# One-hots from a row of 2-byte integers, and the skip projection made in the attention layer's node step

## What is computed

```python
# attention layer: x1 is its result, a row of 256 for each node
x1 = segment_sum(h[src] * alpha[:, :, None], dst, n).reshape(n, H * C1) + gat_bias
x1 = prelu(x1, prelu1_a)
# transformer layer
q = x1 @ Wq + bq;  k = x1 @ Wk + bk;  v = x1 @ Wv + bv
logits2 = einsum("ec,ec->e", q[d2], k[s2]) / 16
alpha2 = segment_softmax(logits2, d2, n)
out = segment_sum(v[s2] * alpha2[:, None], d2, n)
out = out + x1 @ Wskip + bskip
x = x + prelu(out, prelu2_a)
```

## Time and profile before

| | us |
|---|---|
| median of 3 runs | 4608.18 |
| lowest and highest | 4602.61, 4608.73 |
| the profiled execution, its own time | 4611.11 |
| its span | 4609.2 |
| PE, DVE, ACT, POOL busy in it | 3524.1, 2667.7, 742.4, 3235.1 |
| granted TensorE clock, mean | 0.871 |

### The profile page before, as it was taken

The page is one execution under the profiler, slowest core; times in us unless marked ns, Lnnn a source line. Parts: engine busy times, 40 slices in busy tenths (PEclk is TensorE's granted clock), DMA queues, the critical chain, the costliest instruction groups (busy, mean ns, idle before and its releaser), DMA issues. The chain is left out here.

```text
span 4609.2 us, 73629 instructions
## 1 busy us (share of the span) xinstructions
PE 3524.1 (76%) x14587; PEld 2499.9 (54%) x14588; DVE 2667.7 (58%) x10225; ACT 742.4 (16%) x2298; POOL 3235.1 (70%) x3404
## 2 busy tenths in 40 slices
PE   2366666666566666666679999999978899999998
PEld 2244444444344444444456666666656676676666
DVE  8544444444333433344368888887866776776765
ACT  3200000000011111111111111111112322322322
POOL 3477777777677777777677777777727777777762
PEclk7677877777788989989878898999978999999999
DMA  5544444444444444444455555555525555555552
GB/s 165 133 129 132 130 129 131 131 128 129 114 139 136 138 137 138 139 134 138 120 143 155 150 156 151 154 152 155 150 83 141 159 154 152 160 147 145 153 146 73
DMA packets 339313, 639.35 MB, mean 139 GB/s; under 512 B 85419, under 2 KB 218598, under 8 KB 338790
## 3 DMA queue, kind: packets, MB, share of 16 engines
q0 software_dynamic: 159744, 440.25, 35.8%
q1 hardware_dynamic: 159993, 180.48, 12.4%
q10 hardware_dynamic: 19056, 12.87, 1.0%
HBM read 569.33 MB, written 63.99 MB: 137 GB/s over the span
## 5 line engine op out<-in xcount | busy, mean ns | idle before, releaser
L582 POOL DMA_INDIRECT g_G<-t,srcI x1664 | 1587.8, 954 | 507.1 <-issue 507.1
L755 PE MATMUL g_ps<-g_G,g_oh 128*128 128x256 f32 x3328 | 1034.0, 461 | 468.9 <-DMA g_G<-t,srcI 364.4
L755 PEld LDWEIGHTS g_ps<-g_G,g_oh 128*128 128x128 f32 x3328 | 727.9, 228 | 741.0 <-issue 404.6
L1472 POOL DMA_INDIRECT g_G<-t,srcI x832 | 798.5, 960 | 287.7 <-issue 253.3
L881 POOL DMA_INDIRECT g_G<-t,srcI x832 | 806.7, 970 | 253.3 <-issue 251.5
L1813 PE MATMUL g_psA<-g_win,g_ohT 128*128 128x257 f32 x1664 | 548.1, 414 | 105.5 <-issue 46.5
L1574 DVE CUSTOM_DVE_ANT_0 g_junk<-g_G,g_psA 128x257 f32<-128x257 f32 x832 | 348.4, 419 | 288.8 <-PE g_psA L1813 265.2
L1823 PE MATMUL g_ps<-g_G,g_oh 128*128 128x257 f32 x1664 | 509.9, 390 | 0.0
L636 DVE TENSOR_SCALAR g_oh<-iota,g_relx,g_wx 128x128 f32<-128x128 f32 x1664 | 452.2, 364 | 59.1 <-PE g_ps L755 34.0
L1245 PE MATMUL g_ps<-g_Gp,g_oh 128*128 128x264 f32 x1664 | 420.5, 403 | 22.3 <-issue 19.2
L1813 PEld LDWEIGHTS g_psA<-g_win,g_ohT 128*128 128x128 f32 x1664 | 293.0, 197 | 214.9 <-DVE g_L L1574 94.7
(11 more groups left out here) (293 smaller groups left out, 3901.3 us busy)
## 6 DMA issues: line engine op xcount, KB each, us to landing
g_G<-t,srcI POOLq DMA_INDIRECT x3328
g_relb<-relrow SPq DMA_DIRECT2D x104, 512.0 KB
g_own<-t SPq DMA_DIRECT2D x159, 128.0 KB
t<-g_t SPq DMA_DIRECT2D x53, 132.0 KB, 2.7
g_rec<-t SPq DMA_DIRECT2D x53, 132.0 KB
g_rec<-h SPq DMA_DIRECT2D x53, 128.5 KB
x<-g_o SPq DMA_DIRECT2D x53, 128.5 KB, 2.7
g_rec<-x SPq DMA_DIRECT2D x53, 128.5 KB
```

Source lines behind the costliest of these rows:

```text
L582: pool.indirect_dma_start(G[:, b, u, :], None, table, IOA(ap=m.srcI[:, g * UW + u:g * UW + u + 1], axis=0)).then_inc(s_g[b][u // QW], 16)
L755: last = nc.tensor.matmul(ps[:, 0:D], oh[:, u, :], G[:, b, u, :], start=(u == 0), stop=(u == UW - 1))
L1472: pool.indirect_dma_start(G[:, b, u, :], None, m.t4, IOA(ap=m.srcI[:, g * UW + u:g * UW + u + 1], axis=0)).then_inc(s_g[b][u // QW], 16)
```

## The change

Five things change.

1. A second row 0..127, `m.iota16`, in 2-byte integers. The one-hots of all layers (lines 636, 967, 1549) compare this row in place of the float32 one. The output stays float32. The two extra-window helpers keep the old row.
2. In the attention layer's node step PE multiplies the transposed `t4` also by `wsk` (two matmuls) and adds `bskip` (one), into a PSUM bank of its own (`psK`); ACT copies it to `skip`, and SP stores it to a new tensor `m.sk`, a third store in each step.
3. In the same layer two matmuls into `psW` remain of three.
4. The transformer layer's node step loads `m.sk` in place of the own rows. PE transposes the two halves of `an` alone and multiplies by `wv` alone. DVE makes `base = bv * (sum of alpha) + skip` after u = 6 and adds it to `psO` after u = 10; the two halves of the activation then read SBUF.
5. What falls away in `prepare` and `transformer_layer`: the tile `bvs`, the tile `sa` and their memsets. `bv` becomes one of the broadcast rows, `bskip` a row of its own, and one more row block is zeroed in HBM.

```diff
         @block.gpsimd
+            nc.gpsimd.iota(m.iota16[:], [[1, P]], base=0, channel_multiplier=0, allow_small_or_imprecise_dtypes=True)
-            nc.gpsimd.memset(m.bvs[:], 0.0)
...
-            sp.wait_ge(s_set, 1)
-            for r, n in ((0, "bv"), (RB, "bskip")):
-                sp.dma_start(m.bvs[r:r + 1, :], a[n].rearrange("(a n) -> a n", a=1)).then_inc(s_w, 16)
+            sp.dma_start(m.bsk[:], a["bskip"].rearrange("(a n) -> a n", a=1)).then_inc(s_w, 16)
...
-                    nc.vector.tensor_scalar(oh[:, u, :], m.iota[:], relx[:, u:u + 1], wx[:, u:u + 1],
+                    nc.vector.tensor_scalar(oh[:, u, :], m.iota16[:], relx[:, u:u + 1], wx[:, u:u + 1],
                                             ALU.is_equal, ALU.mult).then_inc(s_oh, 1)
...
 def gat_layer(nc, m):
-    LD, ST, NQ = 16, 32, UW // QW
+    LD, ST, NQ = 16, 48, UW // QW
...
-        psW = psb("psW", [P, 512])
+        psW, psK = psb("psW", [P, 512]), psb("psK", [P, 512])
...
                 sp.dma_start(m.qk[bass.ds(start, P), :], q_[:]).then_inc(s_st, 16)
+                sp.dma_start(m.sk[bass.ds(start, P), :], skip[:]).then_inc(s_st, 16)
...
-                    last = nc.vector.tensor_scalar(oh[:, b % 2, u, :], m.iota[:], relx[:, u:u + 1], None, ALU.is_equal)
+                    last = nc.vector.tensor_scalar(oh[:, b % 2, u, :], m.iota16[:], relx[:, u:u + 1], None, ALU.is_equal)
...
-                nc.tensor.matmul(psO[:, 0:RW], m.ones[0:1, :], m.bqk[:], start=False, stop=True).then_inc(s_prod, 1)
+                nc.tensor.matmul(psO[:, 0:RW], m.ones[0:1, :], m.bqk[:], start=False, stop=True)
+                for j in range(2):
+                    nc.tensor.matmul(psK[:, 0:D], lt[:, j, :], m.wsk[:, j, :], start=(j == 0), stop=False)
+                nc.tensor.matmul(psK[:, 0:D], m.ones[0:1, :], m.bsk[:], start=False, stop=True).then_inc(s_prod, 1)
...
-                    for j in range(3):
+                    for j in range(2):
                         nc.tensor.matmul(psW[:], m.ident[:], m.rows[:, 0:2, :], start=True, stop=True)
...
-                nc.scalar.activation(q_[:], psO[:, 0:RW], ACT.Copy).then_inc(s_res, 1)
+                nc.scalar.activation(q_[:], psO[:, 0:RW], ACT.Copy)
+                nc.scalar.activation(skip[:], psK[:, 0:D], ACT.Copy).then_inc(s_res, 1)
...
 def transformer_layer(nc, m):
-                sp.dma_start(own[:], m.t4[bass.ds(start, P), 0:D]).then_inc(s_own, 16)
+                sp.dma_start(skip[:], m.sk[bass.ds(start, P), :]).then_inc(s_own, 16)
...
-                return nc.vector.tensor_scalar(oh[:, b % 4, u, :], m.iota[:], relx[:, b % 2, u:u + 1], None, ALU.is_equal)
+                return nc.vector.tensor_scalar(oh[:, b % 4, u, :], m.iota16[:], relx[:, b % 2, u:u + 1], None, ALU.is_equal)
...
+            def node_base(n):
+                dve.wait_ge(s_own, n * LD + LD)
+                dve.wait_ge(s_x1, n + 1)
+                hold(m, dve)
+                nc.vector.scalar_tensor_tensor(base_[:], m.row("bv"), an[:, D:RW], skip[:], ALU.mult, ALU.add).then_inc(s_base, 1)
+
+            def node_total(n):
+                dve.wait_ge(s_base, n + 1)
+                dve.wait_ge(s_prod, n + 1)
+                hold(m, dve)
+                nc.vector.tensor_tensor(v[:], psO[:, 0:D], base_[:], ALU.add).then_inc(s_out, 1)
...
-                nc.vector.scalar_tensor_tensor(v[:], psO[:, 0:D], 0.0, m.row("prelu2"), ALU.min, ALU.mult)
-                nc.vector.scalar_tensor_tensor(o[:], psO[:, 0:D], 0.0, xa[:], ALU.max, ALU.add).then_inc(s_out, 1)
+                nc.vector.scalar_tensor_tensor(o[:], v[:], 0.0, xa[:], ALU.max, ALU.add)
+                nc.vector.scalar_tensor_tensor(v[:], v[:], 0.0, m.row("prelu2"), ALU.min, ALU.mult).then_inc(s_out, 1)
...
                 pe.wait_ge(s_x1, n + 1)
-                pe.wait_ge(s_own, n * LD + LD)
                 hold(m, pe)
-                for j, src in enumerate((an, an, own, own)):
-                    nc.tensor.transpose(psN[:, j * P:j * P + P], src[:, (j % 2) * P:(j % 2) * P + P], m.ident[:])
-                nc.tensor.transpose(psO[0:1, 256:256 + P], an[:, D:RW], m.ident[:]).then_inc(s_turn, 1)
+                for j in range(2):
+                    last = nc.tensor.transpose(psN[:, j * P:j * P + P], an[:, j * P:j * P + P], m.ident[:])
+                last.then_inc(s_turn, 1)
...
-                for j in range(4):
-                    nc.tensor.matmul(psO[:, 0:D], lt[:, j, :], (m.wv, m.wsk)[j // 2][:, j % 2, :], start=(j == 0), stop=False)
-                nc.tensor.matmul(psO[:, 0:D], sa[:], m.bvs[:], start=False, stop=True).then_inc(s_prod, 1)
+                for j in range(2):
+                    last = nc.tensor.matmul(psO[:, 0:D], lt[:, j, :], m.wv[:, j, :], start=(j == 0), stop=(j == 1))
+                last.then_inc(s_prod, 1)
...
-                nc.scalar.activation(lt[:].rearrange("p j e -> p (j e)"), psN[:], ACT.Copy)
-                nc.scalar.activation(sa[0:1, :], psO[0:1, 256:256 + P], ACT.Copy).then_inc(s_lt, 1)
+                nc.scalar.activation(lt[:].rearrange("p j e -> p (j e)"), psN[:, 0:D], ACT.Copy).then_inc(s_lt, 1)
```

More of the change, by code:

```diff
@@ L43 @@
 QW = 4
-RB = 32
 NLOOP = 8
@@ L1428, in transformer_layer @@
          s_s2, s_cpy, s_bt, s_edge, s_W2, s_M, s_z, s_exp, s_gp, s_xch, s_xoh, s_xop, s_xpa, s_xpu, s_xwin, s_own,
-         s_sum, s_x1, s_turn, s_lt, s_prod, s_out, s_res, s_st) = (sem(n) for n in (
+         s_sum, s_x1, s_base, s_turn, s_lt, s_prod, s_out, s_res, s_st) = (sem(n) for n in (
              "zero", "relx", "oh", "hT", "pa", "pu", "aq", "ok", "agx", "ev", "scol", "pf", "F", "s1", "rt", "run", "Lb", "In",
              "s2", "cpy", "bt", "edge", "W2", "M", "z", "exp", "gp", "xch", "xoh", "xop", "xpa", "xpu", "xwin", "own",
-             "sum", "x1", "turn", "lt", "prod", "out", "res", "st"))
+             "sum", "x1", "base", "turn", "lt", "prod", "out", "res", "st"))
         block = c.enter_context(nc.Block())
@@ L1608, in node_all @@
                 node_scale(n)
+                node_base(n)
+                node_total(n)
                 node_halves(n)
@@ L1743, in body @@
                         differences(k - 1, r1)
+                    if agg and u == 6:
+                        node_base(n2)
+                    if agg and u == 10:
+                        node_total(n2)
                     if agg and u == 11:
@@ L1983, in build @@
         m.x, m.out = a["x"], out
-        m.xa, m.t1, m.t2 = (dram(n, (NW, D)) for n in ("xa", "t1", "t2"))
+        m.xa, m.t1, m.t2, m.sk = (dram(n, (NW, D)) for n in ("xa", "t1", "t2", "sk"))
         m.h0, m.x1 = dram("h0", (NW, RW)), dram("x1", (NW, RW))
```

29 lines of the change are left out of this document (14 added, 15 removed).

## The result

The changed kernel takes 4656.88 us (median of 4 runs, 4647.91 to 4666.16), the kernel before beside it 4607.6 us: ratio 1.0105, 95% interval 1.0091 to 1.0119. It is slower by 1%. In three of the eleven comparisons further down the kernel before took 6144 to 6195 us and not 4603 to 4613, and the others with it, for a cause that stays open; their ratios are given, but what is concluded rests on the other eight. The prediction said 4567 us, in a range of 4535 to 4612. The profiled execution has a span of 4651.7 us, 42.5 us more than before.

The account below looks back on a forecast made before the run. Attention and transformer layers were taken as bound by PE and DVE, POOL near behind. 4609.2 - 62 (transformer) + 21 (attention) = 4568, 4570 for this execution, median 4567 us; one-hots 0; range 4535 to 4612.

Parts of the forecast that it names:

- What bounds the kernel: Graph-convolution layers: POOL's gathers; attention and transformer layers: PE and DVE set the end, POOL near behind at 20.2 us a group.
- Transformer layer, -62 us: Transformer layer: 58 us sooner at the last dot, where POOL becomes the bound, and 4 more in the last node steps.
- Attention layer, +21 us: Attention layer: DVE waits for psF as long as PE's node step grows, 52 x 0.4 us.
- The product: Attention layer's node step: three added matmuls (two by wsk, one for bskip) cost PE 1.57 us together.
- The filling: Attention layer: one of three psW matmuls taken away gives PE back 1.45 us, or 0.9 if at 2.4 GHz.
- The net of +0.4 us a group: Attention layer: added matmuls less the psW matmul, between +0.1 and +0.7 us a group, taken as +0.4.
- PE's clock stays low: Rival, attention layer: with less filling, transposes and product run at 1.2 GHz; 1.65 us a group, 4653 us; chance 0.13.
- the transformer layer's bound: Rival, transformer layer: DVE becomes the bound, gain only 0.6 us a group; 4595 us, median 4592; chance 0.14.
- A contention with POOL: Rival, transformer layer: three DVE steps with two SBUF inputs hold up gathers, 66 us back; 4633 us; chance 0.03.
- The one-hots: All layers: the 2-byte row changes nothing, 0 us; rivals: slower, 4623 us, chance 0.03; faster, 4540 us, chance 0.05.
- Hidden work: Attention layer: ACT's extra copy, 0.39 us, is hidden in its idle time; SP's third store costs 0.
- The chances: Whole kernel: faster than 4599 us 0.76, same 0.08, slower 0.16; the forecast itself 0.60.

Follow-up runs that it names:

- fill2before_c: The kernel before with two psW matmuls in place of three, nothing else: 4604.69 us, ratio 0.9998.
- fill3_again: The changed kernel with the third psW matmul of the attention layer's pass put back: 4687.12 us, ratio 1.0179 to the kernel before.
- mixlate2: The changed kernel with scores spread behind the quarters of sums, skip product issued one pass later, two psW matmuls: 4611.16 us, ratio 1.0013 to the kernel before.
- mix2: The changed kernel with scores spread behind the quarters of sums, two psW matmuls: 1.0116 beside 6185 us; run again, 4681.87 us, 1.0172 to the kernel before.
- late1_b: The changed kernel, scores in their block, skip product issued one pass later, one psW matmul: 4689.34 us, ratio 1.0173 to the kernel before.
- mixlate1: The changed kernel with scores spread behind the quarters of sums, skip product one pass later, one psW matmul: 4605.68 us, ratio 0.9991 to the kernel before.

## Why the prediction was wrong, point by point

- **What bounds the kernel.** "In both layers the users, PE and DVE, set the end; POOL is near behind them": right, but for the attention layer it stopped there, at line 1100's wait for `psF`. The stretch of the whole layer, which the prediction doesn't use, would have said more: TensorE busy for 1012 of 1139 us.
- **Transformer layer, -62 us** (bounds -35 and -70): it was -72, 2 us beyond the bound. The last dot stands at 4618.5 - 3562.6 = 1055.9 us from the first gather, against 1123.9 before: 68 sooner (forecast 66 at most, 58 taken). POOL is the bound, as said. Seen from the users the step is 1047.2 / 52 = 20.1 us, POOL's pace. DVE's wait for `psA` fell from 243.2 us to 95.7 us in a like window of 990 us (forecast: under 150). No run has this part of the change alone; that it holds is read from the two traces. The product is two matmuls and 0.86 us to the next score (forecast: 0.9 to 1.0):

```profile
4310.35 1.03 PE L1811 MATMUL g_psO<-wv,g_lt 128*128 128x256 f32 x4
...
4311.21 0.60 PE L1828 MATMUL g_psA<-g_win,g_ohT 128*128 128x257 f32 x2
```

- **Attention layer, +21 us** (bounds 0 and +36): it was +117. This is the step that failed, in two of its three terms. *The product* was sized rightly as a duration at full clock, 1.57 us against 1.60. *The filling* was credited with 0.9 to 1.45 us of TensorE a pass. Without the product it is worth less than nothing (fill2before_c: busy time +10 us), beside the product 31 us, 0.6 a pass (fill3_again). Its time at half clock doesn't vanish with it; half clock moves on to the work behind. *The clock* was left out of the sum, that is, put at what it was. The net of +0.4 us a group had to be +2.3. In TensorE's busy time that is 34 us of work, 0.65 a group, and 90 us that the durations at full clock don't hold and that the lower clock accounts for, 1.7 a group. Only in the passes whose dip stays at 3.4 us is the forecast's size right: 0.7 us more, 21.10 against 20.40.
- **The rival "PE's clock stays low"** (chance 0.13) is what happened: it gave 4653 us, and 4656.88 was measured. Its sign was "line 1100 waits 2 us"; 134.8 / 51 = 2.6. Its size was right by luck in part: it priced every pass at 1.65 us, with the product's instructions at half speed (ten of them; the two products are twelve), while in fact a third of the passes take nearly 5 us more than the usual 20.3 of before, the first sums running slow as well, a third some 2 us more, and the rest 0.7. The argument against it, "PE has six more instructions right behind", was the mistake: those instructions are what runs at half speed. The sentence of the Trainium skill (TensorE: Matmul & The Clock Gate, Part 1) that activity releases the throttle fits one comparison, a filling less and the clock at 0.81 in place of 0.88 (fill2before_c). It doesn't explain the others: the product added work, and the clock fell from 0.88 to 0.84 (fill3_again); and TensorE, busy for 16.44 of 17.10 us, stayed at 0.50.
- **The other rivals.** DVE isn't the transformer layer's bound: the gathers fill the chain there. A contention with POOL doesn't show: the gathers' mean there is 953 ns against 960, median 946 in both. The one-hots: nothing, as said.
- **Hidden work.** ACT's copy and SP's third store were put at nothing. ACT is busy for 190 of 1256 us, and of DVE's waits in the layer the new store ends one, of 0.8 us; no run leaves them out.
- **The chances.** 0.76 for faster leaned on the sum; the range left the clock case out, which had a chance of 0.13 though the trace showed the clock fall in nearly every pass. An edit that touches instructions lying at half clock should have had it as the first case.

## What to carry to other kernels

Where TensorE's granted clock dips once in every pass, cost an edit by the engine's busy time over the whole stretch and by its clock, not by the durations of the instructions edited. Here a filling of 51 us gave back nothing in one kernel and 31 us in the other, and 85 us of new work brought 29 to 61 us of lower clock. An engine busy for 89% of the layer passed 114 to 146 us of new busy time on as 112 to 148 us of length, though the waits that the profile named were DVE's.

A mean over a layer can hide two kinds of pass: look at single passes, with their length and their clock, before a mean clock is called harmless. Before a matmul is moved, ask where it stands in the ring of waits and where the clock dips: moved a place, the same product gave back 63 us with the scores spread (mixlate2 against mix2) and lost 34 us, a filling less included, with them in a block (late1_b against the changed kernel).

## What the runs showed of the hardware

The granted clock fell while TensorE was hardly idle: at 2940.3, among the score matmuls, after 17.0 us in which TensorE was busy for 15.40; and it stayed at 0.50 for 17.1 us, with TensorE busy for 16.44 of them. The same instructions in another order gave mean clocks of 0.71 and 0.85 (late1_b and mixlate1). What in a pass the clock answers to was not settled. The theory was that the block of scores brings the half clock. mix2, with the scores spread, has stretches of nearly two passes without a dip; but so has the kernel before, with the scores in one block. mix2_b, then the kernel before:

```profile
3072.30:3109.80 37.50, 31.38 (x175) 23.79 (x172) 28.36 (x103) 6.36 (x24) 24.87 (x27) 1.00 0.55 148
```

```profile
2934.30:2968.20 33.90, 29.77 (x164) 22.69 (x162) 29.15 (x106) 5.67 (x20) 25.98 (x27) 1.00 0.62 162
```

An indirect gather takes 946 ns in the median whether DVE has three more instructions with two SBUF inputs a group beside it or not, and a `tensor_scalar` of 128 columns takes 362 ns from a 2-byte source with a 4-byte result, against 364 ns from a 4-byte one.
